# Four graph layers: the message pass by edge tile instead of by pair, with x kept aside in DRAM

## The chip, the cores and the metric

The kernel runs on one core of a Trainium2 chip. The metric is the time of one execution in microseconds on the device, as the median of repeated runs. A NeuronCore has five engines with instruction streams of their own: PE (TensorE, matmuls), DVE (VectorE), ACT (ScalarE), POOL (GpSimd, which issues the gathers here) and SP (SyncE, which issues DMAs). Semaphores alone order them against one another.

## The reference

Four graph layers follow one another over 6250 nodes and 100000 edges, each with a residual and a layer norm: GIN, two GAT convolutions, a relational attention layer and GCN. The part that matters here is the relational layer. It computes, for R = 4 edge types and H = 4 heads of C = 128 columns:

```python
xl = einsum('nf,rfh->nrh', h, W_l) + b_l          # one row of HC = 512 per node and type
xr = einsum('nf,rfh->nrh', h, W_r) + b_r
x = leaky_relu(xl[src, type] + xr[dst, type] + e_feat, 0.2).reshape(E, H, C)
score = einsum('ehc,ehc->eh', x, att[type])
alpha = softmax of score over the edges with one (dst, type), for each head
agg = segment_sum(xl[src, type].reshape(E, H, C) * alpha, dst * R + type).reshape(N, R, H, C)
h_msg = einsum('r,nrc->nc', softmax(gate), agg.mean(axis=2) + bias)
```

The mean over heads and the gate are factors of the weights: per edge the message to `dst` is the sum over four heads of weight times the head's 128 columns of xl. Everything is float32 in this part.

## The kernel before, in words

The edges are sorted by destination. They form 782 edge tiles of 128 (TILES), 49 blocks of 128 nodes (NB). An edge tile whose destinations lie in two blocks is met once for each: a (block, tile) *pair*. There are PAIRS = 832 slots for them, filled in the gin pass by `Plan` (L187), which also makes the index columns for gathers (`idx_l`, `idx_r`, `pidx`, `weight_row`, `psrc`) and, per pair, the register values such as `acc_row` (where the block's sum lies).

The program is a row of blocks of code: gin pass (`aggregate_rows`, L496, its gathers L521), two gat layers (gathers L953, node work L1214 and L1243), relational layer, then ffn and nodes (L2225), gcn pass (`aggregate_rows` again: L521, the hot matrices L568, matmuls L552, adds L589), and the ending. A *hot* matrix has for each of 128 edges a one in the column of its destination; a matmul with it sums edges into nodes. The gin, gcn and gat passes gather into rings of 128 tiles.

The relational layer has three parts. `rel_tables` (L1261) writes `left_table` and `right_table`, rows of 516 float32, in DRAM (L1331). `rel_scores` (L1903, the score pass) gathers right and left rows of each edge tile (L1939), and per tile PE makes edge features and adds the right row (L1975, L1978), DVE adds them to the left row in place (L2029), ACT writes relu of it to `positive` (L2001), and DVE reduces to scores (L2041). SP loads feats and types for groups of tiles (L1956, L1961), and DVE masks them (L2011). The left slot of the ring comes free when ACT is done (`relued`). A softmax over segments runs in chunks beside it. At the end the weights stand in `score`, groups of 128 pairs side by side.

`rel_sum` (L2052, the message pass) is the main subject. All engines pass over the pairs in batches of PAIR = 2:

- POOL gathers 128 rows of `left_table` (264 KB) for each *pair* (L2099) into a ring `msg` of 15 batches, and waits for `product` of the batch that held the slot. It also fetches the weights back by pair (L2086), a group of 128 at a time.
- The last piece of the softmax, `mend_group_vector` (L1896, L1899), makes a group's final weights on DVE; SP and ACT store them to `pair_w` in DRAM (L2075), POOL fetches them by `weight_row`, PE transposes them (L2154) and ACT copies them (L2119), so that a pair's weights are one column for each head.
- DVE makes the hot matrix of each pair (L2202) and for heads 0 and 1 the weighted hot (L2207); ACT makes those of heads 2 and 3 from the plain one (L2143).
- PE does four 128x128x128 matmuls per pair, one for each head, with the weighted hot as weights and the head's columns of the gathered row as data (L2174), summing in PSUM.
- DVE adds the product into the block's 128 columns of `acc`, at an address in a register (L2217), two batches after the hot. DVE, ACT and PE work strictly in the order in which their code is written.

The x rows of the layer stay in SBUF (`x_rows`, 128 x 6272 float32, 3136 KB) through the whole layer, since the block behind it (L2422) adds them.

## Time and profile before

| | us |
|---|---|
| median of 3 runs | 9514.06 |
| lowest and highest | 9514.05, 9531.79 |
| the profiled execution | 9592.08 |
| its span | 9590.1 |
| PE busy, share of the span | 5091.3, 53% |
| DVE busy | 5127.5, 53% |
| ACT busy | 1979.0, 21% |
| POOL busy | 5732.0, 60% |

The span is the time from the first to the last instruction of the profiled execution; 2 us lie around it. Times in the rows further down are microseconds from the start of the span. An engine that isn't busy waits, issues or runs register work. The mean granted clock of TensorE is 0.721 of full speed.

### The profile page before, as it was taken

How to read it: one execution, taken by the hardware profiler on the slowest of the kernel's cores; microseconds unless marked ns; L12 is line 12 of the kernel's file. 1: busy time of each engine (PE TensorE's matmuls, PEld its weight loads, DVE VectorE, ACT ScalarE, POOL GpSimd, SP SyncE). 2: the span in 40 equal slices, each digit the busy share in tenths (PEclk: the TensorE clock that was granted, in tenths of full speed). 3: DMA queues.
4: the chain of work that ended last, by engine and by line, in shares of the span. 5: the costliest groups of instructions: out<-in, count | busy, mean ns of one | idle time of the engine just before them, and what ended most of it. 6: DMA issues, size and time to landing. Idle time of an engine off the chain costs nothing. (4 is left out here: it accounts for less than half of the span.)

```text
span 9590.1 us, 93453 instructions
## 1 busy us (share of the span) xinstructions
PE 5091.3 (53%) x23452; PEld 3483.5 (36%) x23571; DVE 5127.5 (53%) x19615; ACT 1979.0 (21%) x5001; POOL 5732.0 (60%) x5738
## 2 busy tenths in 40 slices
PE   2232333444414444497777777777767777623223
PEld 2222322333313333343333333333356766513222
DVE  3333443444424444676777777777766666723235
ACT  0000022222212222310222222222234444500001
POOL 6666526666446666212666666666566666466675
PEclk7555665555555555698999998898979899855556
DMA  2111122222122222187676776676666666221111
GB/s 67 46 46 47 36 46 61 72 68 68 49 60 70 68 69 68 48 328 268 208 210 210 209 214 207 202 209 204 176 168 176 176 176 176 73 54 46 46 46 47
DMA packets 434195, 1155.57 MB, mean 120 GB/s; under 512 B 106036, under 2 KB 147476, under 8 KB 420744
## 3 DMA queue, kind: packets, MB, share of 16 engines
q0 software_dynamic: 295984, 849.83, 32.3%
q1 hardware_dynamic: 122892, 275.01, 8.5%
q10 hardware_dynamic: 14796, 24.75, 0.8%
q8 instruction: 206, 3.38, 0.1%
q14 instruction: 317, 2.60, 0.1%
HBM read 1016.65 MB, written 132.52 MB: 120 GB/s over the span
## 5 line engine op out<-in xcount | busy, mean ns | idle before, releaser
L953 POOL DMA_INDIRECT gat_ring<-gat_table,psrc_idx x1664 | 1641.9, 987 | 1133.2 <-issue 473.1
L589 DVE TENSOR_TENSOR acc<-acc,bank 128x129 f32 (+1 forms) x1664 | 480.2, 289 | 1480.9 <-remote 1333.1
L1939 POOL DMA_INDIRECT pair<-right_table,idx_r_idx x782 | 790.6, 1011 | 636.8 <-PE bank L1978 195.6
L1148 DVE TENSOR_TENSOR acc<-acc,bank 128x130 f32 x1664 | 482.4, 290 | 1209.0 <-remote 869.9
L2099 POOL DMA_INDIRECT msg<-left_table,pidx_idx x832 | 798.3, 960 | 505.4 <-issue 203.0
L1939 POOL DMA_INDIRECT acc<-left_table,idx_l_idx x782 | 812.0, 1038 | 330.4 <-issue 201.1
L521 POOL DMA_INDIRECT gcn_sum_ring<-gcn_table,src_idx x782 | 787.3, 1007 | 371.8 <-issue 227.6
L521 POOL DMA_INDIRECT gin_sum_ring<-in_x,src_idx x782 | 766.2, 980 | 353.2 <-issue 227.0
L1017 PE MATMUL bank<-gat_ring,gat_hot 128*128 128x130 f32 x3328 | 770.7, 410 | 363.8 <-DVE gat_hot L1137 257.1
L2001 ACT ACTIVATE positive<-acc 128x512 f32<-128x512 f32 x782 | 492.3, 630 | 1981.3 <-DVE acc L2029 1354.6
L1978 PE MATMUL bank<-pair,ident 128*128 128x512 f32 x1564 | 860.0, 633 | 1.0 <-issue 0.2
L1017 PEld LDWEIGHTS bank<-gat_ring,gat_hot 128*128 128x128 f32 x3328 | 686.4, 306 | 414.5 <-DVE gat_hot L1137 206.2
L552 PE MATMUL bank<-gcn_sum_ring,gcn_sum_hot 128*128 x1664 | 343.1, 372 | 809.0 <-issue 575.8
L2029 DVE TENSOR_TENSOR acc<-acc,bank 128x512 f32<-128x512 f32 x782 | 532.7, 681 | 435.6 <-PE bank L1978 257.6
L552 PE MATMUL bank<-gin_sum_ring,gin_sum_hot 128*128 x1664 | 344.9, 375 | 749.4 <-issue 513.5
L1975 PE MATMUL bank<-edge_w,feat 128*128 128x512 bf16 x2282 | 690.6, 412 | 69.3 <-DVE acc L2029 30.3
L2041 DVE CUSTOM_DVE_ANT_0 positive<-positive,bank 128x128 f32<-128x128 f32 x3128 | 706.6, 277 | 19.1 <-issue 17.3
L552 PEld LDWEIGHTS bank<-gcn_sum_ring,gcn_sum_hot 128*128 128x128 f32 x1664 | 296.2, 268 | 855.9 <-issue 855.7
L552 PEld LDWEIGHTS bank<-gin_sum_ring,gin_sum_hot 128*128 128x128 f32 x1664 | 301.1, 272 | 793.5 <-issue 792.4
L1033 ACT ACTIVATE gat_ring<-gat_ring,gat_wt 128x129 f32<-128x129 f32 x1664 | 523.7, 391 | 248.4 <-issue 247.0
L977 PE MATMUL bank<-gat_d_parts,gat_spread 128*128 x1664 | 208.1, 184 | 527.1 <-DVE gat_spread L1053 295.9
L2217 DVE TENSOR_TENSOR acc<-acc,bank 128x128 f32 x832 | 239.1, 287 | 407.2 <-remote 264.2
(554 smaller groups left out, 9362.2 us busy)
## 6 DMA issues: line engine op xcount, KB each, us to landing
gat_place<-local_rows SPq DMA_DIRECT2D x128, 416.0 KB
left_table<-rel_out SPq DMA_DIRECT2D x49, 1032.0 KB, 5.1
right_table<-rel_out SPq DMA_DIRECT2D x49, 1032.0 KB, 3.9
feat<-attr_rows SPq DMA_DIRECT2D x194, 256.0 KB
gat_ring<-gat_table,psrc_idx POOLq DMA_INDIRECT x1664
types<-type_rows SPq DMA_DIRECT2D x98, 256.0 KB
msg<-left_table,pidx_idx POOLq DMA_INDIRECT x832
gin_sum_ring<-in_x,src_idx POOLq DMA_INDIRECT x782
```

The lines of the kernel that those rows point to most:

```text
L521: e.indirect_dma_start(ring[:, at:at + F], None, table[:, :], bass.IndirectOffsetOnAxis(ap=ed["src"][:, i:i + 1], axis=0)).then_inc(*got[b ...
L552: m = e.matmul(sums(b, n), hot_of(b)[:, n * P:(n + 1) * P], ring[:, bass.ds(at[(b * Q + n) % BATCH], width)], start=True, stop=True)
L953: e.indirect_dma_start(ring[:, at:at + TROW], None, table[:, :], bass.IndirectOffsetOnAxis(ap=ed["psrc"][:, i:i + 1], axis=0)).then_inc(*g ...
L1017: m = e.matmul(sums_of(q, n), hot[q % NH][:, n * P:(n + 1) * P], ring[:, at:at + TROW], start=True, stop=True)
L1033: m = e.mul(row, row, wt[:, i % CT:i % CT + 1])
L1939: e.indirect_dma_start(to[j % NG][:, n * LROW:(n + 1) * LROW], None, tab[:, :], bass.IndirectOffsetOnAxis(ap=idx[:, i:i + 1], axis=0)).the ...
L1975: e.matmul(x, m, edge_w[:, q * LROW:q * LROW + HC], start=(q == 0), stop=False)
L1978: e.matmul(x, c["ident"][:, :], side(rights, i), start=False, stop=True).then_inc(*edge_made.up())
L2001: e.activation(positive[i % NA][:, :], side(lefts, i), ACT.Relu, scale=0.8).then_inc(*relued.up())
L2029: e.tensor_tensor(xs, xs, k.psum[bank_x[i % NX]][:, 0:HC], ALU.add).then_inc(*summed.up())
L2041: d = e.tensor_tensor_reduce(out=pos[:, s], in0=pos[:, s], in1=k.psum[bank_a[at % NE]][:, s], scale=1.0, scalar=0.0, op0=ALU.mult, op1=ALU ...
L2099: e.indirect_dma_start(rows[j % NG][:, n * LROW:(n + 1) * LROW], None, left[:, :], bass.IndirectOffsetOnAxis(ap=ed["pidx"][:, i:i + 1], ax ...
```

## The change

The message pass goes by edge tile where it can, in lots of Q = 4:

- POOL gathers each edge tile once (782 gathers, by `idx_l`) into a ring of 3 lots, 12 tiles. The ring lies in the memory of `x_rows`; so SP stores x to DRAM (`x_kept`) at the start of the score pass and loads it back at the end of the message pass. POOL waits for `mixed` of the lot that held the slot.
- ACT multiplies heads 1 and 3 of a row by their weights into a ring `weighted` of RT = 64 tiles (two halves of 128 columns each). DVE multiplies heads 0 and 2 and adds the halves of ACT (scalar_tensor_tensor with both tensor inputs in SBUF).
- Per pair DVE makes one plain hot and PE does two matmuls, one per half, its data at an address in a register (`sum_row`, a new row of the plan). DVE's adds come one lot after the hot.
- There are 208 lots of pairs and 196 of tiles: the last 12 lots have hots, matmuls and adds alone.
- The weights aren't stored and fetched: PE transposes them straight out of `score`. `pair_w`, `pidx` and `weight_row` go.

In the score pass DVE's sum goes to `positive` instead of in place, ACT works in place there, the left slot comes free at `summed`, and DVE instead of ACT waits for `scored`. SP stores x there ahead of the loads of the second group.

```diff
+        (x_out,) = k.begin("x_stored")
...
-                                                    (left, ed["idx_l"], lefts, left_in, relued)):
+                                                    (left, ed["idx_l"], lefts, left_in, summed)):
...
                     if j == 1:
                         soft.sync_keys(e, 0, w["keys"], w["types"])
                         soft.sync_lasts(e, w["last_keys"])
+                        e.dma_start(x_kept[:, :], x_rows[:, :]).then_inc(*x_out.up(16))
...
+                e.wait_ge(*x_out.at(1, 16))
...
-                    if i >= NA:
-                        e.wait_ge(*scored.at(i - NA + 1))
-                    e.activation(positive[i % NA][:, :], side(lefts, i), ACT.Relu, scale=0.8).then_inc(*relued.up())
+                    pos = positive[i % NA][:, :]
+                    e.activation(pos, pos, ACT.Relu, scale=0.8).then_inc(*relued.up())
...
+                        if i >= NA:
+                            e.wait_ge(*scored.at(i - NA + 1))
...
-                        e.tensor_tensor(xs, xs, k.psum[bank_x[i % NX]][:, 0:HC], ALU.add).then_inc(*summed.up())
+                        e.tensor_tensor(positive[i % NA][:, :], xs, k.psum[bank_x[i % NX]][:, 0:HC], ALU.add
+                                        ).then_inc(*summed.up())
...
-        NG, NS, NBANK, FIX, FETCH, TURN = 15, 3, 5, 24, 72, 100
...
+        Q, NR, NH, NBANK, FIX, TURN = HQ, 3, 3, 5, 24, 100
+        LOTS, FULL = PAIRS // Q, -(-TILES // Q)
+        weighted = k.sb("weighted", RT * 2 * F, ctx=late)
+        rows = [x_rows[:, j * LROW:(j + 1) * LROW] for j in range(NR * Q)]
+        hot = [soft.val, soft.ex, soft.step]
+        weight = [soft.near01, soft.tot]
...
+        size = lambda b: min(Q, TILES - b * Q)
+        group_of = lambda i: divmod(i + FRONT, P)
+        row_of = lambda i: rows[i % (NR * Q)]
+        part_of = lambda i, j: weighted[:, (i % RT * 2 + j) * F:(i % RT * 2 + j + 1) * F]
...
+                for i in range(TILES):
+                    b = i // Q
+                    if i % Q == 0 and b >= NR:
+                        e.wait_ge(*mixed.at(b - NR + 1))
...
-                        bass.IndirectOffsetOnAxis(ap=ed["pidx"][:, i:i + 1], axis=0)).then_inc(*got[j % NG].up(16))
+                        row_of(i), None, left[:, :],
+                        bass.IndirectOffsetOnAxis(ap=ed["idx_l"][:, i:i + 1], axis=0)).then_inc(*got[b % NR].up(16))
...
+                e.wait_ge(*mixed.at(FULL))
+                e.dma_start(x_rows[:, :], x_kept[:, :]).then_inc(*x_back.up(16))
+                e.wait_ge(*x_back.at(1, 16))
...
-                for j in range(NBATCH):
-                    g, where = part_of(j * PAIR)
-                    if where == 0 or j == 0:
+                for b in range(FULL):
+                    g, where = group_of(b * Q)
+                    if where == 0 or b == 0:
                         e.wait_ge(*placed.at(g + 1))
-                    if where == TURN + 2 and g + 1 < G:
+                    if where == TURN + Q and g + 1 < SGROUPS:
+                        if g:
+                            e.wait_ge(*mixed.at(b - TURN // Q))
                         put(g + 1)
-                    e.wait_ge(*hot_made.at(j + 1))
-                    if j >= NS:
-                        e.wait_ge(*product.at(j - NS + 1))
-                    for n in range(PAIR):
-                        for h in (2, 3):
-                            m = e.mul(hotw[j % NS][n][:, h * P:(h + 1) * P], hot[j % NS][:, n * P:(n + 1) * P],
-                                      weight_of(j * PAIR + n, h))
-                    m.then_inc(*scaled_s.up())
+                    e.wait_ge(*got[b % NR].at(b // NR * Q + size(b), 16))
+                    free = b * Q + size(b) - 1 - RT + NB
+                    if free > 0:
+                        e.wait_ge(*product.at(-(-free // Q)))
+                    for i in range(b * Q, b * Q + size(b)):
+                        for j in range(2):
+                            h = 2 * j + 1
+                            m = e.mul(part_of(i, j), row_of(i)[:, h * F:(h + 1) * F], weight_of(i, h))
+                    m.then_inc(*scaled.up())
...
-                    e.wait_ge(*weights_in[g % 2].at(g // 2 + 1, 16))
+                    e.wait_ge(*fixed.at(g + 1))
                     if g:
                         e.wait_ge(*placed.at(g))
-                    for h in range(H):
-                        m = e.transpose(k.psum[BANK_T][:, h * P:(h + 1) * P], by_pair[g % 2][:, h * P:(h + 1) * P],
-                                        c["ident"][:, :])
+                    for j in range(RUN):
+                        m = e.transpose(k.psum[BANK_T][:, j * P:(j + 1) * P],
+                                        t["score"][:, g * WIDE + j * P:g * WIDE + (j + 1) * P], c["ident"][:, :])
                     m.then_inc(*turned.up())
...
-                for j in range(NBATCH):
-                    g, where = part_of(j * PAIR)
-                    if where == TURN and g + 1 < G:
+                for b in range(LOTS):
+                    g, where = group_of(b * Q)
+                    if where == TURN and g + 1 < SGROUPS:
                         turn(g + 1)
-                    e.wait_ge(*got[j % NG].at(PAIR * (j // NG + 1), 16))
-                    if j >= NBANK:
-                        e.wait_ge(*added.at(j - NBANK + 1))
-                    e.wait_ge(*scaled_v.at(j + 1))
-                    e.wait_ge(*scaled_s.at(j + 1))
-                    for n in range(PAIR):
-                        for h in range(H):
-                            m = e.matmul(k.psum[j % NBANK][:, n * F:(n + 1) * F], hotw[j % NS][n][:, h * P:(h + 1) * P],
-                                         rows[j % NG][:, n * LROW + h * F:n * LROW + (h + 1) * F], start=(h == 0),
-                                         stop=(h == H - 1))
+                    if b * Q % BATCH == 0:
+                        at = k.regs(ENG.PE, ed["sum_row"], b * Q, BATCH, (RT - 1) * 2 * F)
+                    e.wait_ge(*hot_made.at(b + 1))
+                    e.wait_ge(*mixed.at(min(b + 1, FULL)))
+                    if b >= NBANK:
+                        e.wait_ge(*added.at(b - NBANK + 1))
+                    for n in range(Q):
+                        for j in range(2):
+                            m = e.matmul(k.psum[b % NBANK][:, n * F:(n + 1) * F], hot[b % NH][:, n * P:(n + 1) * P],
+                                         weighted[:, bass.ds(at[(b * Q + n) % BATCH] + j * F, F)], start=(j == 0),
+                                         stop=(j == 1))
                     m.then_inc(*product.up())
...
-                for i in range(NBATCH + 2):
-                    if i < NBATCH:
-                        g, where = part_of(i * PAIR)
-                        if where == 0 or i == 0:
-                            e.wait_ge(*placed.at(g + 1))
+                e.wait_ge(*placed.at(1))
+                for i in range(LOTS + 1):
+                    if i < LOTS:
+                        g, where = group_of(i * Q)
                         if where == FIX and g + 1 < SGROUPS:
                             soft.mend_group_vector(e, g + 1, fixed)
-                        if i >= NS:
-                            e.wait_ge(*scaled_s.at(i - NS + 1))
-                            e.wait_ge(*product.at(i - NS + 1))
-                        mine = ed["local"][:, i * PAIR:(i + 1) * PAIR]
-                        for n in range(PAIR):
-                            m = e.tensor_scalar(hot[i % NS][:, n * P:(n + 1) * P], c["node_iota"][:, :], mine[:, n:n + 1], None,
-                                                ALU.is_equal)
+                        if i >= NH:
+                            e.wait_ge(*product.at(i - NH + 1))
+                        for n in range(Q):
+                            m = e.tensor_scalar(hot[i % NH][:, n * P:(n + 1) * P], c["node_iota"][:, :],
+                                                ed["local"][:, i * Q + n:i * Q + n + 1], None, ALU.is_equal)
                         m.then_inc(*hot_made.up())
-                        for n in range(PAIR):
-                            for h in range(2):
-                                m = e.tensor_scalar(hotw[i % NS][n][:, h * P:(h + 1) * P], c["node_iota"][:, :],
-                                                    mine[:, n:n + 1], weight_of(i * PAIR + n, h), ALU.is_equal, ALU.mult)
-                        m.then_inc(*scaled_v.up())
-                    b = i - 2
+                    if i < FULL:
+                        if where == 0:
+                            e.wait_ge(*placed.at(g + 1))
+                        e.wait_ge(*scaled.at(i + 1))
+                        for t_ in range(i * Q, i * Q + size(i)):
+                            for j in range(2):
+                                h = 2 * j
+                                m = e.scalar_tensor_tensor(
+                                    out=part_of(t_, j), in0=row_of(t_)[:, h * F:(h + 1) * F], scalar=weight_of(t_, h),
+                                    in1=part_of(t_, j), op0=ALU.mult, op1=ALU.add)
+                        m.then_inc(*mixed.up())
+                    b = i - 1
                     if b >= 0:
-                        if b * PAIR % BATCH == 0:
-                            at = k.regs(ENG.DVE, ed["acc_row"], b * PAIR, BATCH, (NB - 1) * ROW)
+                        if b * Q % BATCH == 0:
+                            at = k.regs(ENG.DVE, ed["acc_row"], b * Q, BATCH, (NB - 1) * ROW)
                         e.wait_ge(*product.at(b + 1))
-                        for n in range(PAIR):
-                            into = acc[:, bass.ds(at[(b * PAIR + n) % BATCH], F)]
+                        for n in range(Q):
+                            into = acc[:, bass.ds(at[(b * Q + n) % BATCH], F)]
                             add = e.tensor_tensor(into, into, k.psum[b % NBANK][:, n * F:(n + 1) * F], ALU.add)
                             before = chained.now() if n else added.now() if b else filled.at(1)
-                            add.wait_op(*before, "sem-ge").then_inc(*(added if n == PAIR - 1 else chained).up())
+                            add.wait_op(*before, "sem-ge").then_inc(*(added if n == Q - 1 else chained).up())
 
```

## Rows read from the trace of the kernel before

**Rows 1.** One line's instructions, L2099: durations, first and last start, what ended its idle time.

```profile
L2099 POOL DMA_INDIRECT msg<-left_table,pidx_idx x832: 947/953/1692, 6951.7 to 8239.1; - x167
...
  remote: 169.0, 96
```

**Rows 2.** Timeline where the message pass ends: start, duration, engine, line, idle before.

```profile
8266.44 1.32 SPq L2262 DMA_DIRECT2D ffn_w<-in_L_gnn_Wf  x3
```

**Rows 3.** The page, part 5, the message pass's gathers: busy, mean, idle before, releaser.

```profile
L2099 POOL DMA_INDIRECT msg<-left_table,pidx_idx x832 | 798.3, 960 | 505.4 <-issue 203.0
```

**Rows 4.** Windows: length, busy by engine (instructions), granted clock, DMA share, GB/s.

```profile
7030.00:8240.00 1210.00, 889.24 (x6340) 830.90 (x6338) 806.91 (x3202) 506.41 (x1586) 759.66 (x796) 0.91 0.64 176
8240.00:8266.00 26.00, 25.15 (x208) 24.15 (x208) 24.06 (x101) 15.48 (x49) 0.03 (x1) 1.00 0.07 18
```

**Rows 5.** Timeline of one batch after the last gather of the pass.

```profile
8247.86 0.97 PEld L2174 LDWEIGHTS bank<-msg,soft_step 128*128 128x128 f32 x8
...
8247.90 0.48 DVE L2202 TENSOR_SCALAR rhot<-node_iota,e_local 128x128 f32<-128x128 f32 x2
...
8249.01 0.68 ACT L2143 ACTIVATE soft_top<-rhot,soft_near 128x128 f32<-128x128 f32 x2
...
8249.83 0.47 DVE L2202 TENSOR_SCALAR rhot<-node_iota,e_local 128x128 f32<-128x128 f32 x2
8250.23 0.60 DVE L2207 TENSOR_SCALAR soft_ex<-node_iota,e_local,soft_near 128x128 f32<-128x128 f32 x2
```

**Rows 6.** Timeline of three batches in the middle of the pass.

```profile
7112.95 0.61 DVE L2217 TENSOR_TENSOR acc<-acc,bank 128x128 f32 x2 [2.40 <-remote]
...
7121.72 0.73 PE L2174 MATMUL bank<-msg,soft_step 128*128 128x128 f32 x5 [1.14 <-issue]
...
7121.96 0.61 DVE L2217 TENSOR_TENSOR acc<-acc,bank 128x128 f32 x2 [2.83 <-remote]
```

**Rows 7.** Timeline of the gcn pass at two places (L521 is its gather).

```profile
8990.07 0.68 DVE L568 TENSOR_TENSOR gcn_sum_hot<-node_iota,e_local 128x512 f32<-128x512 f32 x1
8990.25 1.33 POOL L521 DMA_INDIRECT gcn_sum_ring<-gcn_table,src_idx  x1 [0.30 <-issue]
...
9058.95 1.26 DVE L589 TENSOR_TENSOR acc<-acc,bank 128x128 f32 x4 [20.57 <-remote]
```

**Rows 8.** Lines L521 and L953: gathers of the gcn pass and of the first gat layer.

```profile
L521 POOL DMA_INDIRECT gcn_sum_ring<-gcn_table,src_idx x782: 946/952/1467, 8404.8 to 9525.8; - x196
...
L953 POOL DMA_INDIRECT gat_ring<-gat_table,psrc_idx x795: 938/944/1660, 1347.1 to 2499.1; - x199
```

**Rows 9.** Timeline of DVE in the gat layer's end, 128x128 with both inputs in SBUF.

```profile
2655.39 6.37 DVE L1214 SCALAR_TENSOR_TENSOR gat_g<-gat_g,gat_node,acc 128x128 f32<-128x128 f32 x22 [1.42 <-ACT acc L1243]
```

**Rows 10.** Timeline where the pass starts: last mended weights, their way back, first products.

```profile
6991.01 0.95 POOL L2099 DMA_INDIRECT msg<-left_table,pidx_idx  x1 [0.30 <-issue]
6991.03 0.70 DVE L1899 SCALAR_TENSOR_TENSOR score<-soft_pick,score 128x512 f32<-128x512 f32 x1
...
6999.66 0.95 POOL L2086 DMA_INDIRECT soft_near<-pair_w,weight_row  x1 [6.44 <-DMA pair_w<-score]
...
7003.30 1.08 PE L2154 MATMUL bank<-ident,soft_near 128*128 128x128 f32 x4 [20.31 <-DMA soft_near<-pair_w,weight_row]
...
7008.88 1.92 PE L2174 MATMUL bank<-msg,soft_top 128*128 128x128 f32 x8
```

**Rows 11.** Timeline of DVE where a later group's weights are mended.

```profile
7602.13 0.48 DVE L1896 TENSOR_SCALAR soft_pick<-soft_code,soft_ratio 128x512 f32<-128x512 bf16 x1
```

**Rows 12.** The page, part 6, DMA issues: count, KB each, us from issue to landing.

```profile
left_table<-rel_out SPq DMA_DIRECT2D x49, 1032.0 KB, 5.1
```

**Rows 13.** Timeline where the score pass starts.

```profile
4513.16 1.23 DVE L2011 TENSOR_TENSOR feat<-feat,types 128x2048 bf16<-128x2048 bf16 x1 [9.01 <-DMA feat<-attr_rows]
```

**Rows 14.** Waits from 5200 to 6800 in the score pass: us in total, times, longest.

```profile
DVE acc L2029 <- PE bank L1978: 170.8, 117, 4.6
...
POOL acc L1939 <- ACT positive L2001: 64.1, 45, 3.6
```

More of the change, by code:

```diff
@@ L42 @@
 HQ = 4
+RT = 64
 PAIR = 2
@@ L254, in tensor @@
                              stop=True)
-        for g in range(G):
-            m = e.matmul(k.psum[3][:, 2 * G + g:2 * G + g + 1], self.tau_front[0:1, g * P:(g + 1) * P], c["ones"][0:1, 0:1],
-                         start=True, stop=True)
         m.then_inc(*self.taued.up())
@@ L332, in vector @@
         e.tensor_copy(runs(self.psrc), self.field(self.rec, 0)).then_inc(*self.keyed.up())
-        e.tensor_copy(runs(self.ends), self.field(self.rec, 2)).then_inc(*dve.up())
-        e.wait_ge(*self.keyed.now())
-        e.wait_ge(*dve.now())
-        e.scalar_tensor_tensor(out=self.pidx[:, :], in0=self.psrc[:, :], scalar=float(R), in1=self.ends[:, :],
-                               op0=ALU.mult, op1=ALU.add).then_inc(*self.keyed.up())
         to_slots_vector(e, k, ed["local"], (0, 1), self.turned, 4, dve)
@@ L349, in vector @@
                         ).then_inc(*self.ended.up())
-        to_slots_vector(e, k, ed["last"], (6, 7), self.turned, 10, dve)
+        to_slots_vector(e, k, ed["last"], (6, 7), self.turned, 8, dve)
         e.wait_ge(*self.joined.at(1))
@@ L1900, in mend_group_vector, with rel_scores @@
                                    ).then_inc(*(done if r == R - 1 else self.dve).up())
-def rel_scores(k, c, ed, w, tabs, t, acc, soft):
-    left, right, attr_rows, type_rows = tabs[0:4]
+def rel_scores(k, c, ed, w, tabs, t, acc, soft, x_rows):
+    left, right, attr_rows, type_rows, x_kept = tabs
     edge_w, attp, gate = t["edge_w"], t["attp"], t["gate"]
@@ L2047, in _, with rel_sum @@
                 soft.chunk_vector(e, SCHUNKS - 1, 0)
-def rel_sum(k, c, ed, left, pair_w, soft, t, acc):
+def rel_sum(k, c, ed, tabs, soft, t, acc, x_rows):
+    left, x_kept = tabs[0], tabs[4]
     with ExitStack() as late:
-        NG, NS, NBANK, FIX, FETCH, TURN = 15, 3, 5, 24, 72, 100
-        rows = [k.sb(f"msg{j}", PAIR * LROW, ctx=late) for j in range(NG)]
-        hot = [k.sb(f"rhot{j}", PAIR * P, ctx=late) for j in range(NS)]
-        hotw = [(soft.val, soft.top), (soft.ex, soft.same), (soft.step, soft.pen)]
-        by_pair, weight = [soft.near, soft.far], [soft.near01, soft.tot]
-        got = k.slots("pool_dma", NG)
-        weights_in, stored = k.slots("pool_dma_w", 2), k.slots("w_stored", 2)
-        filled, hot_made, scaled_v, scaled_s, product, added, fixed, turned, placed = k.begin(
-            "filled", "hot_made", "scaled_v", "scaled_s", "product", "added", "fixed", "turned", "placed")
-        (brow_made,) = k.begin("biased")
-        LAST, NBATCH = SCHUNKS - 1, PAIRS // PAIR
-        (chained,) = k.begin("dve")
-        gate, brow = t["gate"], t["b_row"][:, 0:F]
-        part_of = lambda i: divmod(i + FRONT, P)
-        weight_of = lambda i, h: weight[part_of(i)[0] % 2][:, h * P + part_of(i)[1]:h * P + part_of(i)[1] + 1]
-        def store(e, g, n):
-            for h in range(H):
-                lo = n * 32 + h * NRUN
-                to = pair_w[g * P + n * 32:g * P + (n + 1) * 32, h * P:(h + 1) * P]
-                e.dma_start(to.rearrange("(u j) q -> u j q", j=RUN),
-                            t["score"][lo:lo + NRUN, g * WIDE:(g + 1) * WIDE].rearrange(
-                                "u (j q) -> u j q", q=P)).then_inc(*stored[g % 2].up(16))
@@ new lines, in rel_sum @@
+        Q, NR, NH, NBANK, FIX, TURN = HQ, 3, 3, 5, 24, 100
[4 more added lines that the diff above has]
+        weight = [soft.near01, soft.tot]
+        got = k.slots("pool_dma", NR)
+        hot_made, scaled, mixed, product, added, fixed, turned, placed = k.begin(
+            "hot_made", "scaled", "mixed", "product", "added", "fixed", "turned", "placed")
```

66 lines of the change are left out of this document (21 added, 45 removed).

## The prediction

> **What bounds the kernel now.** I read the page first, then the line of the message pass's gathers, then windows, then the timeline of single lots. By the page nothing is busy all the time (PE and DVE 53%, POOL 60%, in the table above). The change lies in one stretch of about 1315 us, the message pass from 6951.7 to 8266.4 [rows 1, 2], and touches the score pass before it. In the message pass 832 gathers take 0.95 us of POOL each, and "issue" puts 203.0 us over 665 of them, 0.30 each [rows 1, 3]: 1.257 us per gather if POOL waits for nothing, 5.03 us for four. It doesn't get that. Between 7030 and 8240 POOL issues 796 in 1210 us, 1.52 us each and 6.08 for four [rows 4]; the rest is POOL waiting for a free place in the ring, 169.0 us of it under "remote" [rows 1]. So the consumer sets the pace. Yet no consumer is full: in that window DVE is busy 807 us, PE 889, ACT 506 of 1210, at a granted clock of 0.91 [rows 4].
>
> The timeline says why. When the gathers have stopped, a batch of two pairs takes 1.93 us (8247.90 to 8249.83), with PE's granted clock at 1.00 [rows 4, 5]: 3.9 us for four, faster than POOL's 5.03. While POOL gathers, two batches run at that speed, and at the third DVE stands before its add for 2.4 to 2.8 us; PE shows a gap of 1.14 us inside a batch, where the program has it wait for no one [rows 6]. The period is 9.01 us for three batches (7112.95 to 7121.96), or 1.50 per pair. I can't name the cause from the trace; its effect is that PE's products arrive late. The gcn pass has it worse: there DVE stands 20.6 us before the adds of one lot of four [rows 7]. The passes with lots of four, little work per tile and deep rings pay for it too: 782 gathers of gcn in 1121 us are 5.74 per lot, 795 of the first gat layer in 1152 are 5.80 [rows 8]. So four passes with different consumers reach 5.7 to 6.1 us per four gathers, and none 5.03.
>
> **The change, message pass.** (1) Gathers go by edge tile: 782 instead of 832, at today's pace 50 x 1.52 = 76 us fewer. (2) Per lot of four tiles DVE does 4 hots, 8 scalar_tensor_tensor of 128x128 and 4 adds. Hots: two in 0.40 (8249.83 to 8250.23) [rows 5], 0.8 us. The scalar_tensor_tensor with both inputs in SBUF: 22 in 6.37 us, 0.29 each [rows 9], 2.3 us. Adds: 1.26 for four [rows 7]. Sum 4.4 us, 87% of 5.03, against 3.9 before. (3) ACT: 8 multiplications, each 0.30 behind the one before (two in 0.68, one of them 0.38) [rows 5], 2.4 us. (4) PE: 2 matmuls per pair instead of 4, 16 records per lot; eight records take 0.97 us at 2.4 GHz [rows 5] and 1.92 right after PE's idle time at the pass's start, near 1.2 GHz [rows 10]: 1.9 or 3.8 us. (5) The weights no longer go to DRAM and back. PE and ACT stay below 5.03 either way.
>
> The ring shrinks from 30 pairs to 12 tiles, and POOL waits no longer for PE's product but for `mixed`. A round: the fourth gather is issued 3.8 us after the first; it lands 3.64 us later (by L2086 at 6999.66 and its user on PE at 7003.30, the nearest row for a landing [rows 10]); then 2.4 (ACT), 2.3 (DVE) and some 0.3 of handing over: 12.4 us, against 3 x 5.03 = 15.1. Slack 2.7 us. But DVE works in order: behind its wait for product(b) stand hot(b+2) and the mixing of lot b+2, so a late product now holds `mixed`, and with it POOL. Product(b) may be some 2.5 us late for nothing: PE is done 1.9 us after mixed(b), DVE asks 1.3 + 0.8 + 2.3 = 4.4 us after it. Delays of 2.4 to 2.8 us, as this pass has them, fit in that and the slack, and there are half as many hand-overs per tile; one of 20 us doesn't.
>
> What a lot then costs, L, decides all. Floor 5.03 (POOL); this pass now has 6.08; above that there is no row, so I bound it by the ring's harm under (C). I take **5.8**: passes which hand over lots of four show 5.74 and 5.80 [rows 8], and this one becomes such a pass.
>
> Start: the weights are mended at 6991.73 as now [rows 10], since all before it is unchanged. Then, instead of store, fetch and transposes: four transposes and a copy 1.7 us (1.0 for four transposes by eight records, 0.6 for a 128x512 operation), ACT 2.4, DVE 2.3: mixed(1) at 6998. Only 12 gathers lie before it instead of 30. From there 193 lots x L; +8 us for the last lot's landing, scaling and mixing; +12 for six mended groups, each four times (0.48 + 0.70) us on DVE, 4.8 with gaps [rows 10, 11], of which the slack hides 2.7 (both ends: 0 and 29). Then 12 lots without tiles of their own: hots and adds only, 2.1 us each by DVE (25 us) or 3.8 by PE at the low clock (46): 35. x comes back in that time: 3136 KB, where 1032 KB land in 5.1 us [rows 12], so about 15 us; the 35 us cover it, without them it would cost 15. End: 6998 + 193 x 5.8 + 8 + 12 + 35 = 8172, against 8266.4 [rows 2]. **Gain 94.** In general the gain is 1213 - 193 L.
>
> **Score pass.** The store of x (3136 KB, 15 us by the same row) goes onto SP's queue ahead of the loads types[1] and feats[1], and DVE already waits 9.01 us for feats of this kind at its mask [rows 13]. Between 0 (the loads run beside it) and 15 I take +10. The left slot comes free at `summed` rather than after ACT: POOL waits 64.1 us for ACT in 1600 [rows 14], but behind that stands DVE's own waiting for PE, 170.8 us [rows 14]; between -50 and 0 I take -3. DVE instead of ACT waits for `scored`: its own scores are ahead of it in its order, so mostly nothing, at most +15; +5. Together **+12**. The plan in the gin pass loses seven transposes, seven small matmuls and a few copies that lie beside gin's gathers: 0; without that cover some 3 us gained.
>
> Net 82 us. The profiled execution lasted 9592.1 us around a span of 9590.1, 78 above the median of the runs; 82 us is 0.9% of it, and I take the difference off the median unscaled: 9514 - 82 = 9432, say **9430**.
>
> **A rule that speaks against it.** In gcn a gather that begins inside the hot-making tensor_tensor of L568 (0.68 us, both inputs in SBUF) takes 1.33 us instead of 0.95 [rows 7], while a scalar_tensor_tensor of L1899, 0.70 us and also with two inputs in SBUF, lies over a gather of 0.95 [rows 10]. The Trainium skill ("SBUF — State Buffer", Terms) says that VectorE and GpSimd arbitrate for a shared port pair, locked for the full instruction, and that "the loser **fully blocks**"; "VectorE: DVE Perf Modes" (section Two Vector instructions with no wait between them) has the second of two SBUF tensor inputs read through the interface shared with GpSimd. By that rule all 8 mixing instructions of a lot would stop the gathers; the two rows side with one view each.
>
> **Rivals.** (A) *POOL's own rate is reached*, L = 5.03: fewer hand-overs take the late products away. Gain 242, net 230: 9284. For it: DVE at 87%, delays shorter than the slack; against: no pass does it. (B) *The pace stays*, L = 6.08: net 28, 9486; at L = 6.22 nothing is left. (C) *Slower by the short ring*: long delays of PE's products pass through DVE's order and 12 tiles to POOL. Twelve tiles are 15 us; the rings of the gcn and gat passes hold 128 tiles, 160 us, and a delay of 20 us costs them nothing by itself. It decides from L = 6.22 on; at L = 6.6, 9586. For it: the wait of 20.6 us [rows 7]; against: this pass has 2.4 to 2.8 [rows 6]. (D) *The mixing stops POOL*: if each of 8 adds its 0.29, POOL's lot is 5.03 + 2.3 = 7.3, and the sum 9720; if they stretch gathers in proportion to the row of L568 (0.38 us for 0.68), 1.3 us, L = 6.3 on its own and 9535. Against: L1899. (E) That the round trip of x isn't free, so that the change does not do what it says: +15 at both ends, 9450.
>
> **Chances.** L = 5.5 to 6.05 (the forecast, E within it; its own range 9375 to 9480): 0.43. Below that down to A: 0.20. About 6.1 (B): 0.12, a good half of it within 0.2% (19 us, about what a measurement of this kernel tells from no change). C: 0.17. D: 0.08. Faster 0.66, same 0.09, slower 0.25. Range 9290 (A) to 9590 (C at 6.6).
>
> **What would show it.** The gathers' first to last start over their count gives L. POOL's idle time before them should be put down to the mixing or to "remote". Gathers over 1.0 us beside the scalar_tensor_tensor speak for D; DVE standing over 5 us before adds while POOL stands too, for C. The first mixing should end near 6998, the tail take 25 to 46 us, the score pass be 0 to 25 us longer. The forecast is wrong if PE's products come later as PE has less to do; the granted clock in the pass would then be well under 0.91.

## The result and the profile after

The changed kernel takes 9613.98 us (median of 4 runs, 9610.59 to 9622.73), the kernel before 9519.36: ratio 1.0099, interval [1.0081, 1.0116]. It is 95 us slower, and the forecast was 82 us faster. Two later comparisons of the same pair, on the chips called c and e below, gave 1.0093 [1.0063, 1.0124] and 1.0096 [1.0060, 1.0133]. The profiled execution of before lay 73 us over its median and that of after 3 us under its own, so the two profiles differ by less than the runs do; where exact differences matter below, both kernels are from one chip.

The gathers of the message pass after, from the page's part 5 and from the line by itself (answers to [rows 1, 3]):

```profile
L2080 POOL DMA_INDIRECT x_rows<-left_table,idx_l_idx x782 | 777.0, 994 | 605.5 <-DVE weighted L2185 346.8
```

```profile
L2080 POOL DMA_INDIRECT x_rows<-left_table,idx_l_idx x782: 951/957/2387, 6890.1 to 8234.8; - x196
...
  DVE weighted L2185: 346.8, 73
  issue: 221.9, 708
```

782 gathers instead of 832, and yet 1344.7 us instead of 1287.4. After the ring's first 12 the 770 others go from 6936.5 to 8234.8: L = 6.75 us per lot where 5.8 was forecast, against 6.13 for four gathers of before once its ring of 30 is full. POOL waits 346.8 us for DVE's mixing. DVE in turn waits before its adds, by their own line. The first rows are before, the second after: 209 waits of 1.9 us on average have become 88 of 5.0. The window of the pass shows that DVE isn't short of time (748 of 1210 us busy) and that PE's clock fell (0.70, [rows 4] had 0.91):

```profile
  remote: 264.2, 139
  PE bank L2174: 127.0, 70
```

```profile
  remote: 359.5, 58
  PE bank L2150: 83.0, 30
```

```profile
7030.00:8240.00 1210.00, 533.58 (x2888) 494.20 (x2888) 747.97 (x2915) 438.98 (x1434) 701.78 (x710) 0.70 0.57 156
```

One piece of the timeline has it all (answers to [rows 6]; start, duration, engine, line, idle before):

```profile
7406.53 0.95 POOL L2080 DMA_INDIRECT x_rows<-left_table,idx_l_idx  x1 [5.91 <-DVE weighted L2185]
...
7410.53 2.14 PE L2150 MATMUL bank<-weighted,soft_step 128*128 x16 [0.30 <-issue]
...
7414.69 2.05 PE L2150 MATMUL bank<-weighted,soft_val 128*128 x16 [2.02 <-issue]
...
7418.02 1.25 DVE L2196 TENSOR_TENSOR acc<-acc,bank 128x128 f32 x4 [3.52 <-PE bank L2150]
...
7419.99 2.18 DVE L2185 SCALAR_TENSOR_TENSOR weighted<-x_rows,soft_near,weighted 128x128 f32<-128x128 f32 x8
...
7422.36 3.78 PE L2150 MATMUL bank<-weighted,soft_ex 128*128 x16 [5.62 <-issue]
7422.44 0.95 POOL L2080 DMA_INDIRECT x_rows<-left_table,idx_l_idx  x1 [0.75 <-DVE weighted L2185]
...
7426.23 0.96 POOL L2080 DMA_INDIRECT x_rows<-left_table,idx_l_idx  x1 [0.30 <-issue]
7429.50 1.25 DVE L2196 TENSOR_TENSOR acc<-acc,bank 128x128 f32 x4 [7.33 <-remote]
...
7431.45 2.19 DVE L2185 SCALAR_TENSOR_TENSOR weighted<-x_rows,soft_near,weighted 128x128 f32<-128x128 f32 x8
...
7433.91 0.95 POOL L2080 DMA_INDIRECT x_rows<-left_table,idx_l_idx  x1 [6.73 <-DVE weighted L2185]
```

Each lot's matmuls start when its mixing ends, so the matmuls at 7410.53 and 7414.69 belong to lots n and n + 1. They are done by 7412.67 and 7416.74. DVE's adds of these two lots come at 7418.02 and 7429.50: the products needed 5.4 and 12.8 us to reach DVE. POOL gathers meanwhile from 7406.53 on, twelve without a break and, 0.75 us after them, four more, until the last at 7426.23 has filled the ring. It stands from 7427.19; 2.3 us later the product is through. Then DVE must do adds, hots and mixing, and only at 7433.91, 4.4 us after the product, POOL goes on.

The trace also has the time of most semaphore events, and they say what is late. Behind the first 30 gathers of this pass, 132 of the 183 recorded signals of PE's product came more than 0.5 us after the end of its last matmul. None of the 163 recorded signals of DVE's mixing came more than 0.06 us late, and 3 of ACT's 78 did (at most 1.8 us); each time that POOL had to wait for the mixing it started 0.27 us after the mixing's end. So it is PE's signal that is held here. Of the 132 late ones 85 came while POOL stood for longer than 0.4 us, which it does 26% of the time, by the median 2.1 us after it had stopped; 47 came during gathers or between two of them, as the one at 7417.9 did.

The other steps, from both ends of the pass and the start of the score pass (answers to [rows 2, 10, 13]):

```profile
4474.60 1.22 DVE L2002 TENSOR_TENSOR feat<-feat,types 128x2048 bf16<-128x2048 bf16 x1 [16.97 <-DMA feat<-attr_rows]
```

```profile
6929.83 1.09 PE L2129 MATMUL bank<-ident,score 128*128 128x128 f32 x4 [8.52 <-DVE score L1888]
...
6936.51 1.02 POOL L2080 DMA_INDIRECT x_rows<-left_table,idx_l_idx  x1 [28.89 <-DVE weighted L2185]
```

```profile
8244.44 0.35 SPq L2087 DMA_DIRECT2D x_rows<-x_kept  x1
...
8244.60 2.05 PE L2150 MATMUL bank<-weighted,soft_val 128*128 x16 [0.92 <-issue]
...
8274.42 1.29 SPq L2241 DMA_DIRECT2D ffn_w<-in_L_gnn_Wf  x3
```

### The profile page after: what moved, and what is told of

It reads as the page before. It is cut to its first block and busy times, and to the rows that moved or that the text cites. A ratio compares the mean times of both kernels' runs of the same rounds, so it can differ in the third digit from the quotient of the medians.

```text
span 9608.7 us, 86630 instructions
## 1 busy us (share of the span) xinstructions
PE 4742.2 (49%) x20222; PEld 3142.4 (33%) x20222; DVE 5112.1 (53%) x19512; ACT 1942.2 (20%) x4901; POOL 5717.9 (60%) x5681
## 5 line engine op out<-in xcount | busy, mean ns | idle before, releaser
L2080 POOL DMA_INDIRECT x_rows<-left_table,idx_l_idx x782 | 777.0, 994 | 605.5 <-DVE weighted L2185 346.8
L1992 ACT ACTIVATE positive<-positive 128x512 f32<-128x512 f32 x782 | 492.8, 630 | 1955.3 <-DVE positive L2022 1268.5
L2022 DVE TENSOR_TENSOR positive<-acc,bank 128x512 f32<-128x512 f32 x782 | 532.0, 680 | 445.0 <-remote 236.8
```

The source lines that it names most:

```text
L2022: e.tensor_tensor(positive[i % NA][:, :], xs, k.psum[bank_x[i % NX]][:, 0:HC], ALU.add).then_inc(*summed.up())
L2080: e.indirect_dma_start(row_of(i), None, left[:, :], bass.IndirectOffsetOnAxis(ap=ed["idx_l"][:, i:i + 1], axis=0)).then_inc(*got[b % NR].u ...
```

## The experiments

There are eighteen runs, on five chips called b to f; the chip of the first comparison (a) may be one of the last four. The kernel before ran beside each. L is four times the mean step between gathers once the first ring is full, "waits" what DVE waits in all for products before its adds ("remote" and PE), "to gcn" the time from the pass's first gather to the gcn pass's first, all in us and from one profile each. A median with a star is one run. The kernel before has a median of 9519 on a, 8340 on b, 9515 on c, 9595 on d, 9515 on e and 9620 on f.

| kernel, chip | L | waits | to gcn | median | ratio to before |
|---|---|---|---|---|---|
| before, a | 6.13 | 391 | 1453 | 9519 | |
| after, a | 6.75 | 443 | 1525 | 9614 | 1.0099 |
| before again, b | 5.15 | 174 | 1237 | 8340 | |
| adds two lots behind, b | 5.18 | 0 | 1217 | 8329 | 0.9987 [0.9978, 0.9997] |
| narrow gathers, b | 5.15 | 5 | 1214 | 8314* | |
| PE kept busy, b | 5.19 | 23 | 1239 | 8344* | |
| after, c | 6.83 | 454 | 1539 | 9624 | 1.0093 [1.0063, 1.0124] |
| before, ring of 12, c | 6.03 | 380 | 1443 | 9503* | |
| after, ring of 8, c | 6.36 | 5 | 1453 | 9531* | |
| one input in the mixing, c | 6.46 | 425 | 1465 | 9547* | |
| adds two behind, d | 6.34 | 276 | 1442 | 9602 | 1.0002 [0.9988, 1.0017] |
| narrow gathers, d | 6.64 | 401 | 1502 | 9678* | |
| one fill per lot, d | 6.60 | 354 | 1493 | 9664* | |
| three fills per lot, d | 6.36 | 5 | 1447 | 9613* | |
| after, e | 6.70 | 427 | 1514 | 9594 | 1.0096 [1.0060, 1.0133] |
| adds four lots behind, e | 6.15 | 100 | 1409 | 9493 | 0.9981 [0.9962, 1.0001] |
| adds two behind, two fills, e | 5.94 | 0 | 1362 | 9442 | 0.9934 [0.9913, 0.9955] |
| before, paced, e | 6.08 | 378 | 1443 | 9514 | 1.0002 [0.9984, 1.0021] |
| adds two behind, one fill, f | 6.16 | 186 | 1406 | 9569 | 0.9951 [0.9927, 0.9975] |
| two fills per lot, f | 6.02 | 22 | 1382 | 9559 | 0.9935 [0.9916, 0.9955] |

**The kernel before again, and chip b.** Unchanged.

> The kernel before, unchanged, for a second profile. The first profiled execution lay 78 us over the median of its runs, the one of after lay at its median. If the stages that the change doesn't touch vary by themselves, this profile shows gin, gat and gcn gathers at other rates than 1.423, 1.451, 1.435 us each, by some per cent, and the message pass again at 1.53 us per gather (6.1 per four). If the first profile was an outlier in the message pass itself, this one shows another rate there, down to 1.35.

Gin gathered at 1.306 us each instead of 1.436, the message pass at 1.29 instead of 1.53, and the kernel took 8337 us instead of 9519. On this one chip products are hardly late: 8 of 403 recorded signals came over 0.06 us after the last matmul. So the lateness belongs to the chip (or to what surrounds it): the four others had it. No run tells where it comes from. It isn't noise between runs, which agree within 0.7% on a chip.

**Adds two lots behind.**

```diff
-                for i in range(LOTS + 1):
+                for i in range(LOTS + 2):
-                    b = i - 1
+                    b = i - 2
```

> After, with DVE's adds two lots behind the mixing instead of one. Theory 1 (products arrive late while POOL gathers, and DVE's order hands that on to the ring): each product gets a lot's time more, so a lot of gathers falls from 6.75 us to 5.7-6.2, the kernel is 100 to 200 us faster than after and at or under before (9400 to 9520). Rival 1 (the ring of 12 is too short by itself, whatever DVE waits for): within 20 us of after. Rival 2 (POOL is held up by the mixing's two SBUF inputs): the same as after, gathers of 0.957 us as there.

It met chip b, where there was nothing to win back. L was 5.18: DVE and ACT carry a lot at nearly POOL's rate, as rival A had it. But the kernel before has 5.15 there, and the gain is 12 us.

**Narrow gathers.** The destination is `row_of(i)[:, 0:4]`.

> After, but each gather brings 4 of 516 columns (the rest of each row stays what was there, so the messages are not the reference's): as many gathers and descriptors, 1/129 of the bytes. Theory 1a (it is POOL's issuing of gathers that holds up PE's products): the lot stays at 6.3-6.8 us and DVE's waits before its adds stay above 300 us in all. Theory 1b (it is the traffic of the rows in memory): the lot falls to about 5.1 us and these waits to under 80 us.

L 5.15 on chip b, so nothing about late products, but as a bound: the 516 columns cost nothing there.

**PE kept busy.** Behind each lot's product:

```diff
+                    for _ in range(2 * Q):
+                        e.matmul(k.psum[7][:, 0:F], c["ident"][:, :], c["node_iota"][:, :], start=True, stop=True)
```

> After, with 8 more 128x128 float32 matmuls per lot on PE behind each product (constants into a bank nobody reads), so that PE has as much to do as before the change. Theory 3 (PE with little to do has a lower clock, 0.70 instead of 0.91 in the pass, and its products come later for that): the clock rises to about 0.9 and the lot falls to 6.1 us or less. Theory 1: the clock rises, and a lot falls only by what its matmuls take less, at most 1.7 us where the low clock applied, so to 6.3-6.8.

On chip b the granted clock between 6150 and 7050 was 0.97, against 0.78 with adds two behind and 0.74 with narrow gathers, and L stayed (5.19). It wasn't run on a chip with late products, but two fills per lot (chip f, below) answer theory 3: the clock there is lower still, 0.63, and the lateness is nearly gone. So the low clock doesn't make it.

```profile
7030.00:8060.00 1030.00, 579.40 (x2761) 534.17 (x2762) 739.00 (x2784) 421.02 (x1374) 836.76 (x1028) 0.63 0.65 176
```

**After, again, on chip c.**

> After, unchanged. In the four runs before this one all passes gathered at 1.28 to 1.30 us each, and PE's products weren't late; the kernel before took 8340 us there instead of 9519. Where that holds again: theory 1 (the loss of 95 us came from late products handed on through a short ring) has after within 30 us of before, or up to 40 us faster (50 gathers fewer at 1.3 us are 65 us, the tail of 12 lots gives 20 to 30 back). Rival (the change costs by itself, by its order, its mixing or x's transfers): 30 to 100 us slower than before here too, and slower than the version with adds two lots behind. Where the products are late again (gathers of gin at 1.42): 70 to 120 us slower, as at first.

Late products are back, and with them the whole loss: 1.0093, "to gcn" 96 us more than the kernel before with a ring of 12 on the same chip.

**Before with a ring of 12 pairs; after with a ring of 8 tiles.** `NG` from 15 to 6; `NR` from 3 to 2.

> Before, with the ring of gathered rows cut from 15 batches to 6 (30 pairs to 12). Where products come in time: theory 1 expects the pass at 1.26 to 1.35 us per gather, as with 30 pairs. Where they are late, 1.65 or more instead of 1.53. Rival (ring length doesn't matter): the same rate as with 30 pairs in either case.

> After, with the ring cut from 3 lots of 4 to 2. By the round of 12.4 us that was worked out, a ring of 8 tiles gives 6.2 us per lot (1.55 us per gather) even where products come in time; if the round is really shorter than 10 us, 1.26 to 1.30 remains. Where they are late: 7.5 us per lot or more.

Both went against the forecast and against theory 1 as stated. Cutting the ring of before cost nothing (6.03; one run of 9503 us against a median of 9515), and the shorter ring of after is faster (6.36 against 6.83). The waits at the line of adds are what to look at; the ring of 12 on this chip has 349.8 us of "remote" here and 104.6 of PE:

```profile
  PE bank L2150: 4.8, 9
```

and what POOL waits for before its gathers:

```profile
  DVE weighted L2185: 315.8, 117
```

POOL now stops 117 times, and no product keeps DVE waiting (94 of its 175 recorded signals are still over 0.5 us late, but DVE asks for them later still). With a ring of 12 it stops 79 times for 364.6 us and runs for twelve gathers and more in between, as above. What counts seems to be the unbroken run of gathers; the fills below test it. A ring longer than 12 tiles wasn't run.

**One input in the mixing.** A `tensor_scalar` with mult in place of the `scalar_tensor_tensor`.

> After, with DVE's mixing reduced to a multiplication (one input in SBUF instead of two; the heads that ACT scales are left out of the sum). If the mixing with two SBUF inputs holds up POOL's gathers, their median or mean falls here from 0.957 or 0.99 us, and the pass gets shorter by up to 2 us per lot. If not, both stay within 0.01 us, and the lot within 0.2.

The gathers' median stayed at 0.953 us (mean 0.968 instead of 0.991), L fell by 0.37, more than the 0.2 expected. If each of eight mixing instructions had stopped POOL for its 0.27 us, the gathers alone would have shown 2.2 us per lot; they show 0.09. The rest of the gain I take for the shorter way from product to POOL's restart; that is argued, not shown. Rival D falls.

**Adds two behind and narrow gathers, chip d.** As above.

> After, with DVE's adds two lots behind, once more, since the chip of its first run showed no late products. Where products are late (gin's gathers at 1.42 us): if DVE's order is what hands the delay on to the ring, the lot falls from 6.8 us to 6.2 or less and the kernel to within 40 us of before. If the products are late until POOL pauses, and POOL pauses only where the ring is full, then DVE's waits get shorter but the lot stays at 6.4 us or more.

> After, each gather bringing 4 of 516 columns (the rest of each row stays what was there), once more. Where products are late: if it is POOL's stream of gathers that holds them back, whatever the bytes, the lot stays at 6.3-6.8 us and DVE waits over 250 us before its adds. If it is the traffic of the rows, the lot falls to 5.1-5.3.

The first went between its two expectations: L 6.34, kernel level with before. Against 6.70 to 6.83 on other chips (the change itself wasn't run on d), the order of DVE is worth some 0.4 us per lot, not the whole. The second is clear: with 2 GB/s instead of some 160 on the memory, products are as late as with whole rows. Window and adds:

```profile
7150.00:8200.00 1050.00, 461.18 (x2534) 425.54 (x2532) 654.54 (x2553) 385.06 (x1260) 616.08 (x632) 0.71 0.06 2
```

```profile
  remote: 374.9, 74
```

So it isn't the bytes. The DMA packets fell as well, from 80 per gather to 32, which speaks for POOL's issuing. That the issuing itself does it, and not what remains to be done per gather, is the likeliest reading and not shown.

The first run also has something that `after` hasn't: with DVE no longer waiting in each lot, DVE's own signals are held too.

```profile
7308.23 2.19 DVE L2185 SCALAR_TENSOR_TENSOR weighted<-x_rows,soft_tot,weighted 128x128 f32<-128x128 f32 x8 [1.04 <-issue]
...
7310.97 0.29 DVE L2196 TENSOR_TENSOR acc<-acc,bank 128x128 f32 x1 [0.54 <-remote]
...
7313.72 0.29 DVE L2196 TENSOR_TENSOR acc<-acc,bank 128x128 f32 x1 [2.46 <-remote]
7313.85 3.78 PE L2150 MATMUL bank<-weighted,soft_ex 128*128 x16 [6.55 <-issue]
7313.93 0.95 POOL L2080 DMA_INDIRECT x_rows<-left_table,idx_l_idx  x1 [1.68 <-remote]
```

The mixing ends at 7310.42. PE and POOL, which both wait for it, start 3.4 and 3.5 us later, and between two adds DVE waits 2.46 us for its own signal. In this trace 35 of 142 recorded signals of the mixing are over 0.06 us late. Adds four behind and adds two behind with one fill show the same (32 of 133, 40 of 151).

**Fills on POOL behind each lot.** One of 128x384 (0.43 us), or three:

```diff
+                    if i % Q == Q - 1 and b >= NR:
+                        for _ in range(3):
+                            if paused.n:
+                                e.wait_ge(*paused.now())
+                            e.memset(soft.top[:, 0:384], 0.0).then_inc(*paused.up())
```

> After, with one fill of 128x384 on POOL behind each lot of gathers (0.4 to 0.6 us of POOL, into a tile nobody reads). Theory now (PE's products get through while POOL stands between gathers, and are held back while gathers follow each other): DVE's waits before its adds fall from 407 us to under 150, and the lot from 6.8 to 5.7-6.4 us although POOL has more to do. Rival (only the number of gathers per time counts, or a place free in the ring is what ends it): DVE's waits stay, the lot is 6.8 or longer. Where products are in time: the lot goes from 5.2 to 5.7-5.9 us.

> After, with three such fills behind each lot (1.2 to 1.8 us of POOL). By the theory now DVE's waits before its adds go to nearly nothing, as with the ring of 8 tiles, and the lot is POOL's 5.03 us and the fills, 6.3-6.8. By the rival they stay and the lot is over 7.5 us. Where products are in time: 6.3-6.8.

One fill is too short; with three, POOL has 1.3 us more to do per lot, and the pass is 55 us shorter than with narrow gathers and no pause, on the same chip (the change itself wasn't run there). The kernel is still no faster than before there, 9613 us in its one run against 9595. DVE waits 5 us in all before its adds. L is just what POOL issues: 5.03 + 1.3.

**Adds four lots behind** (six hots instead of three), **two behind with two fills, before paced** (four fills of 128x96, 0.19 us each, behind every fourth gather), and after again, on chip e.

> After, with DVE's adds four lots behind the mixing and a ring of six hot matrices instead of three. If the price is the restart through DVE's order: the mixing goes on without the product, POOL's waits for it fall from 300 us to under 120 and the lot from 6.8 to 5.7-6.1 us, the kernel at least 20 us under before. If POOL then merely gathers on until something else is full and the products are held longer, the lot stays at 6.3 or more, as with two lots behind (6.34), and the kernel within 20 us of before. Where products are in time: 20 to 40 us under before.

> After, with the adds two lots behind and two fills (0.43 us each) on POOL behind each lot. POOL's own rate is then 5.03 + 0.9 = 5.9 us per lot. If a pause of this length lets the products through: the lot is 5.9-6.1, the waits before DVE's adds under 80 us, the kernel 20 to 60 us under before on a chip with late products, and some 120 us over it on one without. If it is too short: 6.3 or more, no better than before.

> Before, with four small fills (128x96) on POOL behind every fourth gather of the message pass, some 0.6 to 1.2 us per four. If gathers in unbroken succession hold back the products in this kernel too: DVE's waits before its adds fall to under half of 252 us, and four gathers take 5.7-6.0 us instead of 6.1, a gain of up to 60 us. If the kernel before paces itself well enough (POOL waits for the product directly and so pauses just then), the pass stays within 20 us.

> After, unchanged, on the same chip as these: 60 to 110 us over before where gin's gathers take 1.42 us each, 0 to 30 us under it where they take 1.30.

Four lots behind, DVE waits 100 us for products, L is 6.15 and the loss is gone: 0.9981, 105 us less to gcn than the change on the same chip. That much DVE's order cost. L isn't 5.03, since products and DVE's signals are still late there and POOL waits 192 us for the mixing. With two fills, DVE never waits for a product and the kernel beats both: 0.9934. Its timeline and its adds:

```profile
7401.43 2.19 DVE L2192 SCALAR_TENSOR_TENSOR weighted<-x_rows,soft_near,weighted 128x128 f32<-128x128 f32 x8 [1.74 <-ACT weighted L2126]
7402.09 0.91 POOL L2089 MEMSET soft_top<- 128x384 f32 x2
7403.16 1.03 POOL L2082 DMA_INDIRECT x_rows<-left_table,idx_l_idx  x1 [0.16 <-issue]
7403.53 1.25 DVE L2203 TENSOR_TENSOR acc<-acc,bank 128x128 f32 x4
...
7403.81 3.67 PE L2157 MATMUL bank<-weighted,soft_val 128*128 x16 [2.10 <-issue]
...
7407.33 2.19 DVE L2192 SCALAR_TENSOR_TENSOR weighted<-x_rows,soft_near,weighted 128x128 f32<-128x128 f32 x8 [1.76 <-ACT weighted L2126]
7407.97 0.91 POOL L2089 MEMSET soft_top<- 128x384 f32 x2
7409.03 1.05 POOL L2082 DMA_INDIRECT x_rows<-left_table,idx_l_idx  x1 [0.15 <-issue]
7409.44 1.25 DVE L2203 TENSOR_TENSOR acc<-acc,bank 128x128 f32 x4
```

```profile
  DVE acc L2203: 0.8, 3
```

Every lot is alike, 5.9 us; adds follow the mixing at once, fills (0.91 us for two) stand between the lots. Pacing the kernel before wins nothing (1.0002), and it doesn't end the lateness: its fills take 0.77 us per four gathers and POOL's waits for products fall to 60 us (272 in the first profile, 252 with a ring of 12), but DVE still waits 378 us. The likely reason is that POOL waits for the product itself there, so it stops just when one is held, and starts again with it (the product that lets DVE go at 7121.96 [rows 6] lets POOL go 0.14 us later); that is argued, and no longer pause was tried.

**Which of the two.** One fill with adds two behind, and two fills with adds one behind, on chip f.

> After, adds two lots behind, one fill of 0.44 us on POOL per lot (POOL's own rate 5.5 us per lot). If the pause needs to be longer than 0.44 + 0.3 us to let a product through: late products remain (DVE waits over 100 us before its adds) and the lot is 6.1-6.5. If the slack of a lot is what mattered: no waits, a lot of 5.5-5.7, 60 to 90 us faster than with two fills.

> After, adds one lot behind as in the change, two fills per lot. If the pause does it: DVE's waits before its adds under 60 us and the lot at 5.9-6.1, the kernel 50 to 80 us under before on a chip with late products. If the slack of a lot did: waits over 150 us and the lot at 6.3 or more.

The pause does it: two fills alone leave 22 us of waits, L 6.02, 0.9935; one fill with the slack leaves 186 and gains less (0.9951, though the two intervals overlap). In the changed kernel the limit lies between 0.44 and 0.9 us of pause per lot beside the usual 0.3.

## Why the prediction was wrong

**The step that failed** is in the part on the ring: "Delays of 2.4 to 2.8 us, as this pass has them, fit in that and the slack". I took the delay for a size of its own. It has none: a product is held while gathers follow each other, and most get through when POOL stands. With the change the product comes up to 12.8 us after its last matmul, where before it was 5.9 at most; DVE stands up to 10.8 us for it, and the mixing behind that wait hands it on to POOL. Why it was short before I can only argue: POOL waits for the product directly there, and the change took that wait away. A ring of 12 pairs leaves it short (5.9 at most), so the ring isn't the reason; no run gives the changed kernel the direct wait back.

The figures that the step used were too small as well: 2.4 to 2.8 us is how long DVE stood. The product itself was 4.4 us late at 7121.96 (its last matmul ended at 7117.57), against the 2.5 that were to be free. And at the lower clock 16 matmuls took 3.78 us instead of the 1.9 in that slack.

L = 5.8 rested on passes with deep rings, and nothing showed that a ring of 12 with DVE's order in between behaves as they do; 6.75 was measured. 193 lots times 0.95 us are 183 us. The measured L holds the mended groups, for which the forecast had 12 us of their own, so 171 are to be taken off the forecast's 82: -89, and the measured change is -95. The sign that the prediction named for (C) came true: DVE stood over 5 us before adds while POOL stood too. The granted clock well under 0.91 (0.70) came too, but two fills at 0.63 show that the clock isn't the cause.

The other terms held, the score pass within 4 to 11 us:
- Restart: from the first transpose (6929.83) to POOL's 13th gather 6.7 us; forecast 6.3 from the mended weights.
- Tail: from the load-back's issue (8244.44) to the next block (8274.42) 30.0 us, forecast 35 within 25 to 46, at 1.9 to 2.4 us per lot at full clock; x was back in time, its traffic over within 12 us.
- Score pass: DVE's first wait for feats rose from 9.01 to 16.97 us, 8 more where +10 was forecast; the pass from first gather to the next pass's first gather took 2466 us on chip c against 2443 in the kernel with before's score pass, and 2460 against 2444 on chip e: 16 to 23 for 12, with runs of the same score pass 14 us apart on chip c.
- DVE's 4.4 us per lot: 0.87 + 2.18 + 1.25 less overlaps, 4.2.

**Rivals.** C had the size (from 9586) and half the mechanism: DVE's order hands late products on, which adds four lots behind undid. Its other half, that 12 tiles are too few, has the wrong sign between 8 and 12 tiles; above 12 it is untested. A's rate is reached only on the chip without late products, where before reaches it too. B's pace, 6.08, wasn't kept either. D is refuted: the mean gather went from 0.960 [rows 3] to 0.994 us, 0.14 us per lot, where 2.3 or 1.3 were in question. The Trainium skill's rule on the shared port ("SBUF — State Buffer", Terms), in which the loser is blocked for the full instruction, doesn't show as a full stop for these float32 instructions with two SBUF inputs.

**What stays open.** Why gathers hold PE's products back, and why one chip of five doesn't do it. Shown for the changed kernel are that bytes don't matter and that a pause of POOL of some 0.9 us per four gathers leaves DVE 0 to 22 us of waits; for the kernel before, 0.77 us didn't do it. PE's signal is held, and where DVE doesn't wait in each lot, DVE's too. One rival is untested: on the four chips the traces lack part of the semaphore events (`after` has 163 of 188 of the mixing); on chip b, with adds two behind, all are there. So what holds the signals may be tied to the recording of the trace itself, and no run here is known to be without it.

## What to carry to other kernels

A delay that a profile shows in a closed loop belongs to the loop: before moving a wait from the signal that is late to one behind it, ask what kept the delay short. Where an engine with a queue of its own (gathers here) is only held by a full ring, a deliberate short pause in its stream can be faster than letting it run, and costs a few lines to try. And measure a change that hangs on such a delay on more than one chip.

## What the hardware showed that was not expected

- The same kernel takes 8340 us on one chip and 9515 to 9620 on the four others; the rate of gathers goes with it, 1.31 against 1.44 to 1.45 us each in gin.
- PE's product can take 12.8 us to reach DVE after its last matmul while POOL gathers without a break; with 0.9 us of pause per four gathers DVE waits 0 to 22 us for products in the whole pass instead of 443.
- Not only PE's signals are held: with the adds two lots behind, PE and POOL started 3.4 and 3.5 us after the end of the mixing that they waited for, where `after` has 0.19 us by the median and 0.27 us each time.
- Gathers of 4 columns issue as slowly as those of 516: POOL 0.98 us each by the mean (0.99 in `after`), L 6.64 where the whole rows had 6.70 to 6.83 on other chips.
